# Two sets of buffers for x1, the gathered expert rows and x3 in the combining stage of a four-stage transformer block

## What is computed

```python
x = x + xattn0(layernorm(x), ctx)            # attention over the context
x = x + moe16(layernorm(x))                  # 16 small experts (192 wide), top 2 per token
x = x + mamba(ctx, z=layernorm(x))           # selective scan over ctx, gated by silu(z)
x = x + moe8(layernorm(x))                   # 8 experts (2048 wide), one top 2 for the whole input
```

## Time and profile before

| | us |
|---|---|
| median of 3 runs | 1610.0 (1607.82 to 1610.88) |
| the profiled execution, its own time | 1611.76 |
| its span, first to last instruction | 1610.0 |
| its mean granted TensorE clock, share of full | 0.925 |
| combining stage, from the first index copy (764.56) to the first matmul of the large experts (884.73) | 120.2 |

### The profile page before, as it was taken

The page is one execution under the profiler, slowest core; times in us unless marked ns, Lnnn a source line. Parts: engine busy times, 40 slices in busy tenths (PEclk is TensorE's granted clock), DMA queues, the critical chain, the costliest instruction groups (busy, mean ns, idle before and its releaser), DMA issues.

```text
span 1610.0 us, 18778 instructions
## 1 busy us (share of the span) xinstructions
PE 1396.8 (87%) x6080; PEld 1030.1 (64%) x6080; DVE 949.6 (59%) x1234; ACT 689.8 (43%) x1255; POOL 754.2 (47%) x559
## 2 busy tenths in 40 slices
PE   6988982599889889888175999999999999999998
PEld 3535531566556556555165787878788787878786
DVE  2767767999999999999584224241423224241413
ACT  4445433356666665665143333333333333333332
POOL 0000000877778778783631444444544445444542
PEclk9898895699999999999555999999999999999999
DMA  3202215477977887862664910020000100010000
GB/s 104 107 31 75 106 54 194 152 251 236 300 269 253 284 272 229 290 198 80 215 216 169 376 56 0 0 66 1 13 0 0 65 13 0 0 52 0 0 0 26
DMA packets 78200, 191.28 MB, mean 119 GB/s; under 512 B 10856, under 2 KB 15752, under 8 KB 77120
## 3 DMA queue, kind: packets, MB, share of 16 engines
q1 hardware_dynamic: 64832, 157.03, 28.5%
q0 software_dynamic: 6400, 20.98, 4.7%
q10 hardware_dynamic: 6912, 12.59, 2.1%
HBM read 152.55 MB, written 38.01 MB: 118 GB/s over the span
## 4 chain that ended last, share of the span: by engine, by line
PE 57%; DVE 25%; issue 9%; ACT 3%; DMA 3%; POOL 2%; ACTq 0%; SPq 0%; DVEq 0%; POOLq 0%
PE decay L1668 22%; PE bank L1657 21%; DVE decay L1235 14%; PE decay L1423 2%; PE bank L1467 2%; DVE XH L1102 2%; PE bank L1527 1%; PE bank L1487 1%; PE bank L1554 1%; PE bank L1430 1%; PE decay L1477 1%; DVE S L1244 1%; PE decay L1473 1%; PE bank L1437 1%; DVE HH L1255 1%
## 5 line engine op out<-in xcount | busy, mean ns | idle before, releaser
L723 POOL TENSOR_TENSOR S<-DTU,Bb 128x1024 f32<-128x1024 f32 x128 | 303.2, 2387 | 105.0 <-PE bank L1527 69.9
L1380 DVE CAST HFH<-HF 128x512 fp32r<-128x512 f32 x128 | 58.9, 460 | 497.2 <-ACT HF L1033 497.2
L805 POOL TENSOR_TENSOR W2L<-W2R,W2H 128x512 fp32r<-128x512 f32 x128 | 172.5, 1347 | 348.1 <-ACT W2H L1028 348.1
L1235 DVE TENSOR_TENSOR_SCAN decay<-decay,S 128x1024 f32<-128x1024 f32 x128 | 292.9, 2288 | 1.7 <-ACT decay L882 1.6
L1657 PE MATMUL bank<-XSH,W1H 128*128 128x512 f32 x512 | 203.4, 397 | 4.2 <-POOL W1L L801 4.2
L1668 PE MATMUL decay<-W2H,HFH 128*128 128x512 f32 x512 | 200.4, 391 | 5.0 <-DVE HFL L1382 5.0
L1657 PE MATMUL bank<-XSH,W1L 128*128 128x512 f32 x512 | 203.2, 397 | 0.0
L1657 PE MATMUL bank<-XSL,W1H 128*128 128x512 f32 x512 | 202.6, 396 | 0.0
L1668 PE MATMUL decay<-W2L,HFH 128*128 128x512 f32 x512 | 199.9, 390 | 0.0
L1668 PE MATMUL decay<-W2H,HFL 128*128 128x512 f32 x512 | 199.6, 390 | 0.0
L801 POOL TENSOR_TENSOR W1L<-W1R,W1H 128x512 fp32r<-128x512 f32 x128 | 171.0, 1336 | 47.7 <-ACT W1H L1019 47.7
(11 more groups left out here) (211 smaller groups left out, 2071.0 us busy)
## 6 DMA issues: line engine op xcount, KB each, us to landing
WGU<-in_L_ffn_gate_w SPq DMA_DIRECT2D x48, 384.0 KB
WGU<-in_L_ffn_up_w SPq DMA_DIRECT2D x48, 384.0 KB
WD<-in_L_ffn_down_w SPq DMA_DIRECT2D x48, 384.0 KB
Bb<-bc_rows SPq DMA_DIRECT2D x32, 512.0 KB, 6.5
Cb<-bc_rows SPq DMA_DIRECT2D x32, 512.0 KB, 8.6
expert_rows<-YT ACTq DMA_DIRECT2D x48, 256.0 KB
W1R<-in_L_ffn_w SPq DMA_DIRECT2D x6, 1024.0 KB, 13.7
W2R<-in_L_ffn_w SPq DMA_DIRECT2D x6, 1024.0 KB, 14.2
```

The costliest lines, as they stand in the source:

```text
L723: pool.tensor_tensor(S[u % NP][:], DTU[:, ds(b, 1), c, :].to_broadcast([P, PAIR, L]), Bb[j][:], ALU.mult).then_inc(dbu_ready, 1)
L805: pool.tensor_tensor(W2L[f % 2][:], W2R[:, ds(e, 1), f, :].rearrange("p e d -> p (e d)"), W2H[f % 2][:].bitcast(F32), ALU.subtract).then_i ...
L1235: dve.tensor_tensor_scan(flat, flat, S[u % NP][:].rearrange("p i l -> p (i l)"), 0.0, ALU.mult, ALU.add).then_inc(scan_done, 1)
```

## The change

All four kinds of buffers are doubled by batch parity, b % 2. Y2_0, X1_0, X1_1 and Y1_0 lie behind a pad, where the small experts' weights lay; Y1_1, Y2_1 and both X3 lie in the lower part, where S, Bb and Cb lay. So x1 of batches 0 and 1 and the gathers of batch 0 wait for `yt_stored` alone, and the gathers of batch 1 for `y_ready` too. The semaphores of the gathers are now one for each parity and count both calls, so that `add_first` waits for all eight DMAs of its batch. In `combine_pool` the two gathers for batch b+2 stand together behind `norm_z(b+1)` and behind the scale and shift of x3 of batch b. Before its first index copy of a batch, `gather_y` waits until the batch before has landed. The wait for the x3 store moves to batch b-2. Outside the stage only the order of XSH and XSL in SBUF changes.

```diff
         g = ExitStack()
-        X1 = sb(g, "X1", [P, T, DM])
         X2 = [sb(g, f"X2_{i}", [P, T, DM]) for i in range(2)]
-        X3 = sb(g, "X3", [P, T, DM])
-        Y1 = sb(g, "Y1", [P, T, DM])
-        Y2 = sb(g, "Y2", [P, T, DM])
+        X3 = [sb(g, f"X3_{i}", [P, T, DM]) for i in range(2)]
...
+        Y1_odd = sb(g, "Y1_1", [P, T, DM])
+        Y2_odd = sb(g, "Y2_1", [P, T, DM])
+        sb(g, "unused", [P, PAD])
+        Y2 = [sb(g, "Y2_0", [P, T, DM]), Y2_odd]
+        X1 = [sb(g, f"X1_{i}", [P, T, DM]) for i in range(2)]
+        Y1 = [sb(g, "Y1_0", [P, T, DM]), Y1_odd]
...
             def combine_transfers(b):
                 if b + 2 < B:
-                    sp.wait_ge(x2_ready, (b + 2) * T)
+                    sp.wait_ge(x2_ready, (b + 1) * T)
+                    sp.wait_ge(x1_loaded, (b + 2) * DMA)
                     load_x1(b + 2)
...
             sp.wait_ge(yt_stored, SLOT_TILES * DMA + DMA)
-            sp.wait_ge(y_ready, B * GB)
-            sp.sem_inc(x3_stored, DMA)
             sp.sem_inc(xt3_stored, DMA)
             load_x1(0)
-            sp.wait_ge(x2_ready, T)
             load_x1(1)
+            sp.wait_ge(y_ready, B * GB)
...
-            def gather_y(b, k, y, count):
+            def gather_y(b, k, count):
-                pool.tensor_copy(pcol[k][:], pos[:, k, ds(b * T, T)]).then_inc(pcol_ready, 1)
-                wait_apart(pool, pcol_ready, count)
+                if b and k == 0:
+                    pool.wait_ge(y_loaded[(b - 1) % 2], ((b - 1) // 2 + 1) * TOP * T * DMA)
+                pool.tensor_copy(pcol[k][:], pos[:, k, b * T:(b + 1) * T]).then_inc(pcol_ready, 1)
+                pool.wait_ge(pcol_ready, count)
...
             def combine_pool(b):
-                if b + 2 < B:
-                    pool.wait_ge(part_ready, (b + 2) * T)
-                    gather_y(b + 2, 0, Y1, b * TOP + (2 * TOP + 1))
                 if b + 1 < B:
                     norm_z(b + 1)
-                if b + 2 < B:
-                    pool.wait_ge(x2_ready, (b + 2) * T)
-                    gather_y(b + 2, 1, Y2, b * TOP + (2 * TOP + 2))
                 scale_and_shift(2 * b + 3 if b + 1 < B else 2 * B, vare3, mean3, rstd3, shift3,
                                 var3_ready, b + 1, rstd3_ready)
+                if b + 2 < B:
+                    pool.wait_ge(part_ready, (b + 1) * T)
+                    gather_y(b + 2, 0, b * TOP + (2 * TOP + 1))
+                    pool.wait_ge(x2_ready, (b + 1) * T)
+                    gather_y(b + 2, 1, b * TOP + (2 * TOP + 2))
             pool.wait_ge(yt_stored, SLOT_TILES * DMA + DMA)
+            gather_y(0, 0, 1)
+            gather_y(0, 1, 2)
             pool.wait_ge(y_ready, B * GB)
-            gather_y(0, 0, Y1, 1)
-            gather_y(0, 1, Y2, 2)
-            pool.wait_ge(part_ready, T)
-            gather_y(1, 0, Y1, 3)
+            gather_y(1, 0, 3)
+            gather_y(1, 1, 4)
             norm_z(0)
-            pool.wait_ge(x2_ready, T)
-            gather_y(1, 1, Y2, 4)
             for b in range(B):
                 combine_pool(b)
...
             def add_first(b):
-                dve.wait_ge(x1_loaded, b * DMA + DMA)
-                dve.wait_ge(y_loaded[0], b * (T * DMA) + T * DMA)
+                dve.wait_ge(x1_loaded, max(b + 1, 2) * DMA)
+                dve.wait_ge(y_loaded[b % 2], (b // 2 + 1) * TOP * T * DMA)
...
             def add_second(b):
-                dve.wait_ge(y_loaded[1], b * (T * DMA) + T * DMA)
...
             def combine(b):
                 if b + 1 < B:
                     add_second(b + 1)
-                dve.wait_ge(x3_stored, b * DMA + DMA)
+                x3 = X3[b % 2]
+                if b >= 2:
+                    dve.wait_ge(x3_stored, b * DMA)
+                    dve.wait_ge(xn3_ready, b * T - T)
...
+                dve.wait_ge(x3_ready, b * T + T)
                 if b:
                     dve.wait_ge(xn3_ready, b * T)
...
+                statistics(x3, vare3, mean3, var3_ready)
                 if b + 2 < B:
                     add_first(b + 2)
```

More of the change, by code:

```diff
@@ L20 @@
 WQ = 4
+PAD = 6200
 class Steps:
@@ L276, in build_program @@
         XS = sb(h, "XS", [P, K // 2, L])
-        XSH = [sb(h, f"XSH{i}", [P, K, L], F32R) for i in range(2)]
-        XSL = [sb(h, f"XSL{i}", [P, K, L], F32R) for i in range(2)]
+        XSH = [sb(h, "XSH0", [P, K, L], F32R)]
+        XSL = [sb(h, "XSL0", [P, K, L], F32R)]
+        XSH.append(sb(h, "XSH1", [P, K, L], F32R))
+        XSL.append(sb(h, "XSL1", [P, K, L], F32R))
         h.close()
@@ L362, in build_program @@
         yt_stored = sem("yt_stored")
+        pcol_ready = sem("pcol_ready")
         x1_loaded = sem("x1_loaded")
-        pcol_ready = sem("pcol_ready")
-        y_loaded = [sem(f"y{k}_loaded") for k in range(TOP)]
+        y_loaded = [sem(f"y_loaded{i}") for i in range(2)]
         part_ready = sem("part_ready")
@@ L591, in load_x1 @@
             def load_x1(b):
-                sp.dma_start(X1[:], x1_dram[ds(b * T, T)].rearrange("t p d -> p t d")).then_inc(x1_loaded, DMA)
+                sp.dma_start(X1[b % 2][:], x1_dram[b * T:(b + 1) * T].rearrange("t p d -> p t d")).then_inc(x1_loaded, DMA)
             def load_xs(tb, i):
@@ L601, in combine_transfers @@
                 if b + 2 < B:
-                    sp.wait_ge(x2_ready, (b + 2) * T)
+                    sp.wait_ge(x2_ready, (b + 1) * T)
+                    sp.wait_ge(x1_loaded, (b + 2) * DMA)
                     load_x1(b + 2)
                 sp.wait_ge(x3_ready, (b + 1) * T)
-                sp.dma_start(x3_dram[b * T:(b + 1) * T].rearrange("t p d -> p t d"), X3[:]).then_inc(x3_stored, DMA)
+                sp.dma_start(x3_dram[b * T:(b + 1) * T].rearrange("t p d -> p t d"), X3[b % 2][:]).then_inc(x3_stored, DMA)
                 if b == 1:
@@ L614, in _ @@
             sp.wait_ge(yt_stored, SLOT_TILES * DMA + DMA)
-            sp.wait_ge(y_ready, B * GB)
-            sp.sem_inc(x3_stored, DMA)
             sp.sem_inc(xt3_stored, DMA)
             load_x1(0)
-            sp.wait_ge(x2_ready, T)
             load_x1(1)
+            sp.wait_ge(y_ready, B * GB)
             for b in range(B):
                 combine_transfers(b)
-            sp.wait_ge(x3_stored, B * DMA + DMA)
+            sp.wait_ge(x3_stored, B * DMA)
             sp.wait_ge(lidx_ready, 1)
@@ L746, in _ @@
                     gather(0, j + 2)
-            def gather_y(b, k, y, count):
-                pool.tensor_copy(pcol[k][:], pos[:, k, ds(b * T, T)]).then_inc(pcol_ready, 1)
-                wait_apart(pool, pcol_ready, count)
+            def gather_y(b, k, count):
[3 more added lines that the diff above has]
+                pool.wait_ge(pcol_ready, count)
                 for t in range(T):
                     pool.indirect_dma_start(
-                        out=y[:, t, :], out_offset=None, in_=y_dram,
-                        in_offset=bass.IndirectOffsetOnAxis(ap=pcol[k][:, t:t + 1], axis=0)).then_inc(y_loaded[k], DMA)
+                        out=(Y1, Y2)[k][b % 2][:, t, :], out_offset=None, in_=y_dram,
+                        in_offset=bass.IndirectOffsetOnAxis(ap=pcol[k][:, t:t + 1], axis=0)).then_inc(y_loaded[b % 2], DMA)
             def scale_and_shift(n, var, mean, rs, sh, ready, count, done):
@@ L987, in combine_act @@
                 for t in range(T):
-                    act.activation(ZN3[:, t, :], X3[:, t, :], ACT.Identity, scale=rstd3[:, t:t + 1],
+                    act.activation(ZN3[:, t, :], X3[b % 2][:, t, :], ACT.Identity, scale=rstd3[:, t:t + 1],
                                    bias=shift3[:, t:t + 1]).then_inc(xn3_ready, 1)
@@ L1289, in add_first @@
             def add_first(b):
-                dve.wait_ge(x1_loaded, b * DMA + DMA)
-                dve.wait_ge(y_loaded[0], b * (T * DMA) + T * DMA)
+                dve.wait_ge(x1_loaded, max(b + 1, 2) * DMA)
+                dve.wait_ge(y_loaded[b % 2], (b // 2 + 1) * TOP * T * DMA)
+                x1 = X1[b % 2]
                 for t in range(T):
-                    dve.scalar_tensor_tensor(X1[:, t, :], Y1[:, t, :], rwt[:, 0, b * T + t:b * T + t + 1], X1[:, t, :],
+                    dve.scalar_tensor_tensor(x1[:, t, :], Y1[b % 2][:, t, :], rwt[:, 0, b * T + t:b * T + t + 1], x1[:, t, :],
                                              ALU.mult, ALU.add).then_inc(part_ready, 1)
             def add_second(b):
-                dve.wait_ge(y_loaded[1], b * (T * DMA) + T * DMA)
                 for t in range(T):
                     dve.wait_ge(part_ready, b * T + (t + 1))
-                    dve.scalar_tensor_tensor(X2[b % 2][:, t, :], Y2[:, t, :], rwt[:, 1, b * T + t:b * T + t + 1], X1[:, t, :],
-                                             ALU.mult, ALU.add).then_inc(x2_ready, 1)
+                    dve.scalar_tensor_tensor(X2[b % 2][:, t, :], Y2[b % 2][:, t, :], rwt[:, 1, b * T + t:b * T + t + 1],
+                                             X1[b % 2][:, t, :], ALU.mult, ALU.add).then_inc(x2_ready, 1)
```

(15 more changed lines are left out.)

## The result

The changed kernel takes 1637.3 us (median of 4 runs, 1635.4 to 1639.3) against 1610.1 us before (4 runs): 27.1 us more, a ratio of 1.0171 with an interval of 1.0156 to 1.0186. The forecast was 1633, between 1625 and 1642. The profiled execution has a span of 1637.5 us and a time of 1639.27.

What follows compares the result with a forecast made beforehand. Bound: a chain of waits in the combining stage, no engine full. The last batch's chain comes 21.0 us late, plus 2.0 for contention: +23 us on 1610.0, so 1633, range 1625 to 1642.

Steps and rivals of the forecast that it cites:

- contention: Gathers landing late beside stores and x1 loads on the DMA engines: +1.4 us for batch 2, +0.6 for batch 3.
- largest term: Gathers of batches 2 and 3 issue on POOL behind x3's statistics while VectorE idles: 15.1 us exposed, twice.
- Rival 3: Gathers of batches 2 and 3 land before x3's statistics are done, so VectorE never waits: 1601 us; chance 0.03.
- neighbour row: Last Y2 gather of batch 2 before the change, beside a 1 MB store: 5.09 us against 3.65, +1.4.
- Rival 1: Heavier contention where store, x1 load and gathers meet: 5.9 us more for each of two landings, 1643 us; chance 0.12.
- head start: First index copy released by the last expert-row store: 0 to 3.5 us earlier, 2.5 taken, copy at 762.1.
- rival without a head start: Last store's semaphore fires about when y_ready does, so head start is 0: 1635.5 us; chance 0.06.
- joint wait: add_first waits for all eight gathers, 13.68 us from index copy; first add no longer overlaps them, 10.7 us in all.
- tail: From ZN3 of batch 3 to the first large-expert matmul nothing changes: 22.80 us.

Runs made afterwards that it cites:

- gathers_first: Changed kernel with the two gathers of batch b+2 moved on POOL ahead of norm_z(b+1) and x3's scale and shift: 1607.1 us.
- first_early: gathers_first with x1 of batch 3 loaded earlier on SP, near 795: 1602.1 us.
- hold_stores: Changed kernel, but SP waits before storing XT3 of batches 0 and 1 until the gathers of batch b+2 have landed: 1630.1 us.
- hold_all: hold_stores, with the x1 load of batch 2 also waiting until the gathers of batch 1 have landed: 1628.1 us.
- early_start_alone: Kernel before, single buffers, with X1 and Y1 placed where the small experts' weights lay, so batch 0 loads earlier: 1605.1 us.
- split_waits: Changed kernel with four gather semaphores instead of two, so add_first and add_second each wait only for their own four DMAs: 1628.0 us.
- first_split_early: Changed kernel with gathers of batch b+2 first on POOL, four gather semaphores, and x1 of batch 3 loaded early: 1596.8 us.

## Why the prediction was right, and where it was off

The sign, the place and the mechanism were right, and the time lies in the range, 4 us above the figure; that it is not further off is in part luck, as the account of contention below shows. Step by step, the profile of the changed kernel against the forecast:

| step | forecast | measured |
|---|---|---|
| first index copy | 762.1 | 759.92 |
| rows of batch 0 used | 775.8 | 773.90 |
| rows of batch 1 used | 789.5 | 789.92 |
| product of batch 0 | 798.0 | 798.41 |
| rows of batch 2, from its index copy | 13.68 + 1.4 | 18.23 |
| product of batch 1 | 829.6, with contention 831.0 | 834.51 |
| rows of batch 3, from its index copy | 13.68 + 0.6 | 16.15 |
| product of batch 2 | 861.2, with contention 863.2 | 868.51 |
| ZN3 of batch 3 | 882.9, with contention 884.9 | 890.04 |
| first matmul of the large experts | 905.7, with contention 907.7 | 912.93 |

**The largest term**, two gathers of 15.1 us with nothing of VectorE over them, was right: the index copies stand behind x3's shift, and putting them ahead gives 30 us back (gathers_first), the whole loss within the error of measurement. Rival 3 said what would happen with the other order, 1601, 9 us below the kernel before. That order alone is not clearly faster than the kernel before; with the x1 load moved as well it is 5.6 us faster (1602.1 against 1607.7, first_early). The rival's working had left out that the x1 load of batch 3 stands on SP behind the store of XT3.

**The term that was mis-sized is contention.** I booked 2.0 us: 1.4 for batch 2, 0.6 for batch 3, none for batch 1. Against the 13.4 us of a batch with no neighbour (hold_stores) the runs show 4.8, 2.7 and, for batch 1, 2.6 (15.99 in the changed kernel), 10.1 in all; against the 13.61 of the same batch in hold_all it is 2.4. Two errors are in it. The neighbour row, the last gather beside the x3 store at +1.4, stood for one transfer; batch 2 had two. And for batch 1 I looked only at the start of the stage: the x1 load of batch 2, which the change itself allows earlier, is issued at 779.4, in the middle of the gathers of batch 1. Rival 1 (5.9 for each of two batches, 1643) was the same mechanism at too high a price for each, but its sum, 11.8, lay nearer to these 10.1 than the 2.0 that I booked. Counted as in the table, the four landings (13.98, 15.99, 18.23, 16.15) took 7.7 us more than the sum had for them.

**The head start** was taken too small, and this hid part of it: the first index copy comes 2.06 us after the issue of the last store, where it was 5.76 before (764.56 - 758.80), a gain of 3.7 where I took 2.5, just beyond my upper bound of 3.5. The store itself also came 0.9 us earlier in this profile (757.86 against 758.80). Together this took 2.2 of the 7.7 us back, and ZN3 of batch 3 comes 5.1 us after its forecast. early_start_alone confirms the head start by 4.4 us. The rival without a head start falls.

**The joint wait** costs what the working had it cost (9.2 of 10.7). It and the neighbour of batch 1 are why the early start brings so little: counted from the last store's issue, product 0 comes after 40.55 us (798.41 - 757.86), against 41.12 before (799.92 - 758.80). Without the joint wait it comes after 35.88 (split_waits), without the neighbour after 38.21 (hold_all).

**The rest of the sum** held: from the first product to x3's statistics and back to an index copy, 798.41 to 807.78, 9.37 us against 7.99 + 1.44 = 9.43; adds and statistics, 826.01 to 834.51, 8.50 against 8.49; tail, 890.04 to 912.93, 22.89 against 22.80. One reading of the diff ahead of the prediction was wrong without weight: the wait for the x3 store did not move to batch b-2. For batches 2 and 3 its value, two and three stores, still takes in the store of the batch just before. VectorE waits 1.08 us there ahead of the product of batch 3 (877.67), while ScalarE is still busy with batch 2.

The Trainium skill's rule to double-buffer so that DMA overlaps with compute (Trainium Kernel Development and Optimization, section "Best Practices") is borne out only where the gathers stand first on POOL: there a batch costs VectorE 16.47 us (798.50 to 814.97 in gathers_first, 790.25 to 806.72 in first_split_early). With the single buffers of before it cost 16.99 (799.92 to 816.91). In the changed kernel the buffers are doubled and 27 us are lost; by these runs a second buffer allows the overlap, and the issuing queue's order decides whether it takes place.

## What to carry to other kernels

A second buffer is worth something only if the transfer into it is issued earlier: for each one, look at what stands before it on the queue that issues it, and ask whether the consumer has any work left at that moment. A semaphore that counts two transfers makes the first consumer wait for both. And a transfer that is not urgent costs time if it is put beside one that is waited for: price it with the number of neighbours it will really have, those that the change itself brings forward among them.

## What the runs showed of the hardware that I had not expected

- **The price of a neighbour.** The last gather of a batch (128 rows of 2 KB) is used 3.7 to 3.9 us after its issue starts when it is alone (817.33 to 821.06 in hold_stores; 3.9 in hold_all). With one transfer of 1 MB beside it, issued from another engine, this is 5.8 to 7.2 over the profiles (783.69 to 789.92 and 853.52 to 860.03 in the changed kernel, 6.2 and 6.5). With two it is 8.6 (817.43 to 826.01, one case). All eight gathers of a batch take 13.4 to 13.6 us from index copy to use with no neighbour, 15.6 to 17.0 with one and 18.2 with two. It matters when the neighbours come: the two x1 loads of batches 0 and 1, issued together with the first gather (759.96), leave batch 0 at 13.98 us (759.92 to 773.90). The table of short stretches of the changed kernel has the DMA engines at 0.53 while hardly anything but the gathers runs, and at 0.89 after the two transfers have joined:

```profile
808.00:817.00 9.00, 7.64 (x36) 7.24 (x36) 0.00 (x0) 4.70 (x8) 6.82 (x8) 0.50 0.53 152
817.20:826.00 8.80, 2.62 (x13) 2.52 (x12) 0.00 (x0) 0.21 (x2) 0.95 (x1) 0.50 0.89 316
```

  The Trainium skill, DMA: Bandwidth & Descriptors, section "Issuing engines are not separate DMA queues", says that DMAs from different engines run on the same 16 DMA engines and interleave; these runs agree. The fit on the same page, section "Anatomy of one DMA — SWDGE (gpsimd) path", 2.0 us plus bytes over 436e3, gives 2.6 us for such a gather as an estimate. The 3.7 to 3.9 measured with no neighbour are longer, and they hold the issue of 0.95 us too.
- **A store's completion.** In every profile in which the start waits for it, the index copy follows the issue of the last 256 KB store by 2.06 to 2.08 us (757.86 to 759.92, 756.30 to 758.38). The time contains both the store's completion and what POOL takes to go on.
- **The stage ahead moves by itself.** That store is issued at 758.80, 757.86, 756.95, 754.68 and 752.59 in kernels whose first two stages are the same. Differences of a few us between two profiles should be taken from a common event, not from the start.
